# Expert layer: the last layer norm moved beside the eighth expert's products, its rows patched by gather and scatter

## The chip, the cores and the metric

The kernel runs on one core of a Trainium2 chip. The metric is the device time of one execution in microseconds (us). Engines: PE is TensorE (its weight load is PEld), DVE is VectorE, ACT is ScalarE, POOL is GpSimd; SP issues DMAs, and POOL issues the indirect ones (gathers and scatters by a list of row numbers).

## The reference

```
x = x + cross_attention(layernorm(x), ctx)          # 4 x 1024 tokens of 256
hidden = layernorm(x)
# mixture of experts on hidden, 8 experts, each token goes to its best two
scores = softmax(hidden @ wg); gates, idx = top_k(scores, 2); gates /= sum(gates)
pos = place of the token in its expert's list (1280 places an expert)
h = silu(disp @ fc1_w.T + fc1_b)                    # 256 -> 1024
y = h @ fc2_w + fc2_b                               # 1024 -> 256
res = hidden + sum over the two experts of gate * y[pos]
x = x + (res - mean(res)) * rsqrt(var(res) + 1e-5) * ln_gamma + ln_beta
```

All data are 32-bit floats; the 4096 tokens are 32 tiles of 128 rows.

## The kernel before, in words

**Stages.** Attention fills most of the first 290 us and leaves `X` (residual rows, in SBUF, 32 tiles) and two copies in DRAM of the normalised rows: `xn_rows`, from which experts gather, and `sum_rows`, onto which their results are added. Routing then makes `slot_ids`: for each slot the row numbers to gather and to scatter (empty places scatter to rows beyond the 4096th).

**Expert stage.** Each of 8 experts has `SPE` = 5 slots of 256 places, so there are `NST` = 40 slots, numbered 0 to 39; slots 35 to 39 are the eighth expert's. `expert_steps` runs a step c = 0 to 42 on PE, ACT and DVE, each engine taking its own list in order. In step c PE transposes the gathered rows of slot c+1, makes the first product of slot c (`fc1`), and then the second product of slot c-1 (`fc2`, two halves of 128 rows, each into its own bank, `YB` and `YB`+1). A half may only begin when DVE has read the bank of the slot before (`y_made`). ACT makes `xT_hi` (`rows_hi`), silu (`hraw`), and multiplies the results of slot c-2 by their gates (`scale_results`, `y_scaled`). DVE adds the bias to the results of slot c-2 (line 1687), makes `xT_lo` of slot c+1 (line 1669), splits `hraw` into `h_hi` (line 1699) and `h_lo` (line 1701), and splits weights of the next expert. A product is three matmuls (`mm3`, lines 897 to 899) of such high and low parts. Slots that lie wholly or by half beyond the expert's tokens skip their products (line 1235 stands in).

**POOL** runs its own loop: in turn `st` it gathers the rows of slot `st`+4 (line 599, two indirect DMAs), scatters slot `st`-2 with addition onto `sum_rows` (line 611, two) and, up to `st` = 31, adds `beta_sb` to a tile of `X`. SP loads the next expert's weights (`w1raw`, `w2raw`).

**Last stage.** When all scatters have landed, SP loads `sum_rows` into `res` in nine DMAs and layer norm runs over 8 groups of 4 tiles (`QT`, `NQ`): ACT makes the statistics of the first two tiles, DVE those of the last two (lines 1725, 1729); POOL raises the variance to the power -0.5 (line 658); DVE (lines 1735, 1741) or ACT (line 887), POOL (gamma, line 663) and DVE (line 1747) scale the rows and add `X`; SP stores `z` to `out`.

Of the kernel before, what the change touches and what calls it, by code (L numbers as in the profile page):

```python
# [5 lines left out]
def xattn_moe_kernel(nc, x, ctxT, wqT, bq, wkT, bk, wvT, bv, woT, wo, bo, boT, wg, w1T, b1T, w2, b2, gamma, beta, out):  # L6
# [50 lines left out]
    sum_rows = nc.dram_tensor("sum_rows", [N + 4 * P, D], f32, kind="Internal").ap()  # L57
    x_t = x.rearrange("(t p) d -> p t d", p=P)
# [24 lines left out]
    with root:  # L83
        def sb(name, shape, dt=f32, where=root):
# [20 lines left out]
        my_row = sb("my_row", [P, 1])  # L105

# [85 lines left out]
        w1_hi, w1_lo = sb("w1_hi", [P, 2, DC, HID], f32r, M), sb("w1_lo", [P, 2, DC, HID], f32r, M)  # L192
        w2_hi, w2_lo = sb("w2_hi", [P, 2, HJ, D], f32r, M), sb("w2_lo", [P, 2, HJ, D], f32r, M)
# [12 lines left out]
        res = sb("res", [P, NT, D], f32, C)  # L206
        z = sb("z", [P, NT, D], f32, C)
        unused, squares = sb("unused", [P, 2, D], f32, C), sb("squares", [P, 2, D], f32, C)
        st_d, mv_d = sb("st_d", [P, NT, 6], f32, C), sb("mv_d", [P, NT, 2], f32, C)
        m16_d, nmu_d, var_d, vare_d, rstd_d, nmr_d = (sb(n, [P, NT], f32, C)  # L210
                                                      for n in ("m16_d", "nmu_d", "var_d", "vare_d", "rstd_d", "nmr_d"))
        eps_d, zero_d = sb("eps_d", [P, QT], f32, C), sb("zero_d", [P, QT], f32, C)
        C.close()

        def halves_in_order():

            for k in range(1, NQ + 2):
                if k <= NQ:
                    yield QT * (k - 1) + 2
                if k >= 2:  # L220
                    yield QT * (k - 2)
# [9 lines left out]
        for name in (  # L231
# [7 lines left out]
            "xT_hi_made h_made y_scaled w_hi_made z_made mean16_made act_stats_made "  # L239
# [7 lines left out]
            "h_hi_made h_lo_made y_made st3_made mv3_made var3_made nmr_made z_scaled_dve out_made"  # L247
# [19 lines left out]
        stored = dma_sem("stored")  # L267

# [110 lines left out]
        def _(sp):  # L379
# [46 lines left out]
            sp.wait_ge(scattered[0], 32 * (NST // 2))  # L426
            sp.wait_ge(scattered[1], 32 * (NST // 2))
# [4 lines left out]
            for g, a in enumerate(halves_in_order()):  # L432
                sp.wait_ge(sem("out_made"), g + 1)
                sp.dma_start(out_t[:, a:a + 2, :], z[:, a:a + 2, :]).then_inc(stored, 16)
            sp.wait_ge(stored, 16 * (NT // 2))


        @block.gpsimd
        def _(pool):
# [27 lines left out]
            g.memset(ones_f[:], 1.0).then_inc(sem("zero_made"), 1)  # L467
            pool.wait_ge(sem("masks_made"), 3)
# [134 lines left out]
            def scatter(st):  # L603

                if within(st, NST):
# [3 lines left out]
                    for q in range(2):  # L609
# [3 lines left out]
                                             compute_op=ALU.add).then_inc(scattered[u], 16)  # L613

# [39 lines left out]
            for k in range(NQ + 1):  # L654
                if k < NQ:
                    quad = slice(QT * k, QT * (k + 1))
                    pool.wait_ge(sem("var3_made"), k + 1)
                    g.tensor_tensor(rstd_d[:, quad], vare_d[:, quad], minus_half[:, 0:QT], ALU.pow)\
                        .then_inc(sem("rstd3_made"), 1)
                if k >= 1:  # L660
                    for t in (QT * (k - 1), QT * (k - 1) + 1):
                        pool.wait_ge(sem("z_made"), 2 * (k - 1) + t % QT + 1)
                        g.tensor_tensor(z[:, t, :], z[:, t, :], gamma_sb[:], ALU.mult).then_inc(sem("z_scaled"), 1)
# [3 lines left out]
        def _(act):  # L667
# [166 lines left out]
            def scale_results(gq, c):  # L834
                if within_st(gq, c):
                    e = 2 * gq + c // SPE
                    for q in range(2):
                        act.wait_ge(sem("y_made"), 2 * (10 * gq + c) + q + 1)
                        y = y_sb[:, c % 2, q, :]
                        a.activation(y, y, ACT.Copy, scale=xg[:, c % XR, q, ds(D + e, 1)]).then_inc(sem("y_scaled"), 1)  # L840

            def expert_step(gq, c):
                rows_hi(gq, c + 1)
                if within_st(gq, c):
                    st = 10 * gq + c
# [7 lines left out]
                scale_results(gq, c - 2)  # L853
                e, s = 2 * gq + c // SPE + 1, c % SPE
# [6 lines left out]
            def first_two(k):  # L861

                if k < NQ:
                    a0 = QT * k
                    for t in (a0, a0 + 1):
                        res_loaded(act, t)
                        a.activation(unused[:, t % 2, :], res[:, t, :], ACT.Copy, scale=1.0 / (16 * D),
                                     accum_out=m16_d[:, t:t + 1]).then_inc(sem("mean16_made"), 1)
                    act.wait_ge(sem("mean16_made"), 2 * (k + 1))
                    a.activation(nmu_d[:, a0:a0 + 2], m16_d[:, a0:a0 + 2], ACT.Copy, scale=-16.0)\  # L870
                        .then_inc(sem("act_stats_made"), 1)
                    for t in (a0, a0 + 1):
# [4 lines left out]
            first_two(0)
            first_two(1)
            for k in range(NQ):
                first_two(k + 2)  # L880
                act.wait_ge(sem("rstd3_made"), k + 1)
                for t in (QT * k, QT * k + 1):
                    a.activation(nmr_d[:, t:t + 1], nmu_d[:, t:t + 1], ACT.Copy, scale=rstd_d[:, t:t + 1])\
                        .then_inc(sem("nmr_made"), 1)
                act.wait_ge(sem("nmr_made"), 2 * (k + 1))
# [912 lines left out]
```

## Time and profile before

| what | value |
|---|---|
| median of 3 runs | 766.76 us (766.38 to 767.35) |
| span of the profiled execution | 769.2 us (no other time is listed for it) |
| PE busy | 680.1 us, 88% of the span |
| DVE busy | 564.4 us, 73% |
| ACT busy | 406.3 us, 53% |
| POOL busy | 430.1 us, 56% |
| DMA | 64.10 MB, mean 83 GB/s |

The busy time of an engine says how much work it has over the whole span; which of them sets the end differs by stage and is read from the chain of waits and from windows of the span. Times of rows are counted from the start of the span.

### The profile page before, as it was taken

The page shows a single profiled execution, that of the slowest core. Times are in us where ns is not written, and L with a number is a line of the kernel's source. Part 1 is how long each engine was busy: PE and PEld are TensorE (multiplying, and loading weights), DVE is VectorE, ACT ScalarE, POOL GpSimd, SP SyncE. Part 2 cuts the span into 40 slices and gives each one's busy share as a digit, 9 for nine tenths or more (in the row PEclk, how much of TensorE's full clock was granted, in tenths as well). Part 3 has the DMA queues.
Part 4 walks back from the last instruction along what each step waited for, and adds up shares of the span by engine and source line. Part 5 has one row for each costly group of instructions (what it writes and reads, how often), then busy time and mean ns, then how long its engine had stood idle before and what let it go on. Part 6 is the DMA issues. An engine that isn't in the chain of part 4 may idle for free.

```text
span 769.2 us, 15696 instructions
## 1 busy us (share of the span) xinstructions
PE 680.1 (88%) x5592; PEld 649.1 (84%) x5592; DVE 564.4 (73%) x1198; ACT 406.3 (53%) x955; POOL 430.1 (56%) x547
## 2 busy tenths in 40 slices
PE   5999999999999834999999999999999999999500
PEld 4789999998988723999999999999999999999500
DVE  5589898988888797665565679777696666854187
ACT  3356555555555594454454467455464454643185
POOL 6744665565564334436445558766576554632456
PEclk9699999999999955999999999999999999999855
DMA  9501101011010122434344446544455343322484
GB/s 295 176 15 43 42 28 43 30 41 43 29 43 29 42 85 65 149 84 94 51 107 69 81 106 123 125 96 73 98 123 114 46 101 52 58 29 28 64 266 150
DMA packets 55764, 64.10 MB, mean 83 GB/s; under 512 B 9472, under 2 KB 50944, under 8 KB 55552
## 3 DMA queue, kind: packets, MB, share of 16 engines
q0 software_dynamic: 15360, 21.31, 17.1%
q1 hardware_dynamic: 39616, 41.64, 16.6%
q8 instruction: 55, 0.90, 0.5%
q14 instruction: 29, 0.24, 0.1%
q10 hardware_dynamic: 704, 0.01, 0.0%
HBM read 39.22 MB, written 23.72 MB: 82 GB/s over the span
## 4 chain that ended last, share of the span: by engine, by line
PE 81%; DVE 11%; issue 3%; DMA 2%; ACT 1%; POOL 1%; POOLq 0%; SPq 0%; DVEq 0%; ACTq 0%
PE banks L897 18%; PE banks L899 18%; PE banks L898 18%; PE banks L1039 8%; PE banks L1025 5%; PE banks L1013 5%; PE banks L1171 2%; PE banks L1075 1%; PE banks L920 1%; DVE oh_lo L1485 1%; PE banks L942 1%; DVE oh_id L1481 1%; DVE z L1741 1%; DMA res<-sum_rows 1%; DVE z L1735 1%
## 5 line engine op out<-in xcount | busy, mean ns | idle before, releaser
L611 POOL DMA_INDIRECT sum_rows<-y_sb,slot_ids x80 | 131.4, 1643 | 162.1 <-ACT y_sb L840 145.4
L850 ACT ACTIVATE hraw<-banks,b_now 128x256 f32<-128x256 f32 x320 | 132.2, 477 | 90.3 <-PE banks L899 80.5
L897 PE MATMUL banks<-xT_hi,w_hi 128*128 128x256 f32 x560 | 161.6, 289 | 1.7 <-ACT xT_hi L822 1.7
L899 PE MATMUL banks<-xT_hi,w_lo 128*128 128x256 f32 x560 | 158.5, 283 | 0.0
L898 PE MATMUL banks<-xT_lo,w_hi 128*128 128x256 f32 x560 | 158.4, 283 | 0.0
L897 PE MATMUL banks<-w_hi,h_hi 128*128 128x256 f32 x528 | 148.8, 282 | 1.3 <-issue 1.3
L898 PE MATMUL banks<-w_lo,h_hi 128*128 128x256 f32 x528 | 148.6, 281 | 0.0
L899 PE MATMUL banks<-w_hi,h_lo 128*128 128x256 f32 x528 | 148.5, 281 | 0.0
L1701 DVE TENSOR_TENSOR h_lo<-hraw,h_hi 128x512 fp32r<-128x512 f32 x160 | 114.6, 716 | 5.5
L1699 DVE CAST h_hi<-hraw 128x512 fp32r<-128x512 f32 x160 | 77.5, 485 | 45.8 <-ACT hraw L850 44.6
L897 PEld LDWEIGHTS banks<-xT_hi,w_hi 128*128 128x128 f32 x560 | 106.3, 190 | 2.2 <-issue 2.1
L599 POOL DMA_INDIRECT xg<-xn_rows,slot_ids x80 | 89.8, 1122 | 30.3 <-issue 29.4
L898 PEld LDWEIGHTS banks<-xT_lo,w_hi 128*128 128x128 f32 x560 | 106.4, 190 | 0.2 <-issue 0.2
L899 PEld LDWEIGHTS banks<-xT_hi,w_lo 128*128 128x128 f32 x560 | 106.2, 190 | 0.0
L897 PEld LDWEIGHTS banks<-w_hi,h_hi 128*128 128x128 f32 x528 | 99.4, 188 | 1.8 <-issue 1.8
L899 PEld LDWEIGHTS banks<-w_hi,h_lo 128*128 128x128 f32 x528 | 99.4, 188 | 0.0
L898 PEld LDWEIGHTS banks<-w_lo,h_hi 128*128 128x128 f32 x528 | 99.4, 188 | 0.0
L738 ACT ACTIVATE probsT<-banks 124x384 f32<-124x384 f32 (+1 forms) x128 | 55.8, 436 | 70.9 <-PE banks L1025 70.8
L822 ACT ACTIVATE xT_hi<-banks 128x512 fp32r<-128x512 f32 x40 | 24.1, 602 | 114.2 <-PE banks L1171 106.3
L1039 PE MATMUL banks<-VB,probsT 124*128 124x51 f32 (+2 forms) x640 | 82.7, 268 | 0.0
L1039 PEld LDWEIGHTS banks<-VB,probsT 124*128 124x128 f32 x640 | 81.4, 192 | 0.0
L574 POOL TENSOR_TENSOR rstd<-var,minus_half 128x1 f32<-128x1 f32 x32 | 17.6, 550 | 96.3 <-DVE var L1580 96.3
(216 smaller groups left out, 1442.7 us busy)
## 6 DMA issues: line engine op xcount, KB each, us to landing
w1raw<-in_w1T SPq DMA_DIRECT2D x8, 1024.0 KB
w2raw<-in_w SPq DMA_DIRECT2D x8, 1024.0 KB
xn_rows<-xn SPq DMA_DIRECT2D x32, 128.0 KB, 1.8
sum_rows<-xn SPq DMA_DIRECT2D x32, 128.0 KB, 1.8
out<-z SPq DMA_DIRECT2D x16, 256.0 KB, 2.2
res<-sum_rows SPq DMA_DIRECT2D x7, 512.0 KB, 8.5
X<-in_x SPq DMA_DIRECT2D x2, 1280.0 KB, 12.1
xg<-xn_rows,slot_ids POOLq DMA_INDIRECT x80
```

Of the source, the lines that this page charges most:

```text
L599: g.indirect_dma_start(xg[:, st % XR, q, :], None, xn_rows, bass.IndirectOffsetOnAxis(ap=slot_ids[:, st, 0, q:q + 1], axis=0), bounds_chec ...
L611: g.indirect_dma_start(sum_rows, bass.IndirectOffsetOnAxis(ap=slot_ids[:, st, 1, q:q + 1], axis=0), y_sb[:, u, q, :], None, bounds_check=N ...
L738: a.activation(probsT[:, j0:j0 + w, :].rearrange("r j q -> r (j q)"), banks[0:JW, PT, 0:w * P], ACT.Copy).then_inc(sem("pT_made"), 1)
L850: a.activation(hraw[:, j // 2, j % 2, :], banks[:, j // 2, (j % 2) * 256:(j % 2 + 1) * 256], ACT.Silu, bias=b1_now[:, (c // SPE) % 2, j:j ...
L897: t_.matmul(o, a_hi, b_hi, start=first, stop=False)
L898: t_.matmul(o, a_hi, b_lo, start=False, stop=False)
L899: return t_.matmul(o, a_lo, b_hi, start=False, stop=last)
L1013: m = t_.matmul(banks[:, 2 * f + h, 0:KC], qq[rows, f, qs], kk[rows, ds((2 * b + f) * KH + h * KC, KC)], start=(n == 0), stop=(n == 2))
L1025: m = t_.transpose(banks[0:JW, PT, (j - j0) * P:(j - j0 + 1) * P], probs[:, 1 - u, f * KH + j * JS:f * KH + j * JS + JW], ident[:])
L1039: m = t_.matmul(banks[:, PV, f * VW + a_:f * VW + a_ + n_], probsT[:, NJ * f + j, :], VB[:, ds(((2 * b + f) * NJ + j) * VW + a_, n_)], sta ...
L1699: v.tensor_copy(hi, raw).then_inc(sem("h_hi_made"), 1)
L1701: v.tensor_tensor(lo, raw, hi.bitcast(f32), ALU.subtract).then_inc(sem("h_lo_made"), 1)
```

## The change

The last stage is taken apart. (1) The rows of the seven first experts' sums (`sum_rows` after slot 34) are loaded and normalised in the steps c = 36 to 40 of the eighth expert (`FIRST_SLOT` = 36): `wave_step(k)` on DVE, two groups of four tiles a step, `first_normalised` on ACT, `deviations` and `first_scaled` on POOL, and all rows are stored to `out`. (2) The eighth expert's results are not scattered. For its 10 half slots POOL gathers the sums of those rows (`gather_sums`) and the rows of `X` with beta (`gather_rest`, from `rest_rows`, a new copy in DRAM that SP writes during the expert stage); DVE adds gate times result to the gathered sums (`patch_sum`), normalises them after its last step (`patch_begun`, `patch_done`), and POOL scatters them over their rows of `out` (`scatter_patch`) after all the other stores. (3) Besides: for slots 35 to 39 ACT makes `h_hi` instead of DVE, and the bias `b2` enters as a matmul with a row of ones; the statistics of two tiles come from one instruction over 512 interleaved elements, for all tiles on DVE; the buffers for this lie where weights lay.

```diff
@@ sync
+                sp.wait_ge(sem("beta_added"), QT * e)
+                sp.dma_start(rest_t[:, ds(QT * (e - 1), QT), :], X[:, ds(QT * (e - 1), QT), 0:D]).then_inc(rests_stored, 16)
...
+            for u in range(2):
+                sp.wait_ge(scattered[u], 32 * ((SL + 1 - u) // 2))
...
             for n, (a, b) in enumerate(RES_LOADS):
-                sp.dma_start(res[:, a:b, :], sum_t[:, a:b, :]).then_inc(load_res[n], 16)
+                sp.dma_start(wave(a, b), sum_t[:, a:b, :]).then_inc(load_res[n], 16)
...
+            for n, a in enumerate(pairs_in_order()):
+                store_pair(n, a)
             sp.wait_ge(stored, 16 * (NT // 2))
+            sp.wait_ge(patched, 16 * 2 * SPE)
@@ gpsimd
-                if within(st, NST):
+                if within(st, SL):
...
+                if 0 <= st - SL + 2 < SPE:
+                    gather_rest(st - SL + 2)
...
+            for u in range(2):
+                pool.wait_ge(scattered[u], 32 * ((SL + 1 - u) // 2))
+            for m in range(SPE):
+                gather_sums(m)
+            deviations(0)
+            deviations(1)
+            for k in range(NQ):
+                deviations(k + 2)
+                first_scaled(k)
+            patch_deviations(0)
+            patch_deviations(1)
+            pool.wait_ge(stored, 16 * (NT // 2))
+            for m in range(SPE):
+                scatter_patch(m)
+                patch_deviations(m + 2)
@@ scalar
+                if c == SL + 1:
+                    scale_results(c - 2)
...
+                        if st >= SL and j % 2 and j > 1:
+                            activation_hi(st, j // 2 - 1)
...
+                k = 2 * (c - FIRST_SLOT - 1)
+                if 0 <= k < NQ:
+                    first_normalised(k)
+                    first_normalised(k + 1)
@@ tensor
+                        if e == LAST:
+                            pe.wait_ge(load_b2, 16)
+                            pe.wait_ge(sem("zero_made"), 3)
+                            t_.matmul(o, ones_row[:], b2_sb[0:1, e, :], start=True, stop=False)
@@ vector
+            def quad_begun(k):
+                a = QT * k
+                for n in (2 * k + 1, 2 * k):
+                    pair_stats(n)
+                dve.wait_ge(sem("st3_made"), 2 * k + 2)
+                v.tensor_scalar(var_d[:, a:a + QT].rearrange("p (a b) -> p a b", b=2), st_d[:, 2 * k:2 * k + 2, :, 2],
+                                1.0 / D, EPS_LN, ALU.mult, ALU.add).then_inc(sem("var3_made"), 1)
+                for t in (a + 2, a + 3):
+                    z = row_of(wave(t, t + 1))
+                    v.scalar_tensor_tensor(z, z, st_d[:, t // 2, t % 2, 1:2], gamma_sb[:], ALU.subtract, ALU.mult)\
+                        .then_inc(sem("z_scaled_dve"), 1)
...
+            def wave_step(k):
+                if k < NQ:
+                    quad_begun(k)
+                    quad_begun(k + 1)
+                    first_bias(k)
+                    last_done(k)
+                if k >= 2:
+                    first_done(k - 2)
+                    first_done(k - 1)
+                if k < NQ:
+                    first_bias(k + 1)
+                    last_done(k + 1)
...
+            def patch_sum(c):
+                if c == SL:
+                    dve.wait_ge(sums_gathered, 16 * 2 * SPE)
+                for q in range(2):
+                    dve.wait_ge(sem("fc2_done" if q else "fc2_half_done"), c + 1)
+                    r = row_of(patch(2 * (c - SL) + q, 2 * (c - SL) + q + 1))
+                    v.scalar_tensor_tensor(r, banks[:, YB + q, 0:D], xg[:, c % XR, q, D + LAST:D + LAST + 1], r,
+                                           ALU.mult, ALU.add).then_inc(sem("y_made"), 1)
...
             def expert_step(gq, c):
...
+                elif within_st(gq, c - 2):
+                    patch_sum(c - 2)
                 rows_lo(gq, c + 1)
...
+                if c == FIRST_SLOT:
+                    dve.wait_ge(sem("beta_added"), NT)
+                k = 2 * (c - FIRST_SLOT)
+                if 0 <= k < NQ + 2:
+                    wave_step(k)
...
+            patch_begun(0)
+            for m in range(SPE):
+                if m + 1 < SPE:
+                    patch_begun(m + 1)
+                patch_done(m)
```

`first_bias` is one small DVE instruction that waits for `deviations` of its group, `last_done` two of 128x256 behind it, `first_done` one of 128x512 that waits for `first_scaled`. `patch_begun` is a statistics instruction over 128x512, a small one, and two of 128x256; `patch_done` two of 128x256 that wait for `patch_deviations`.

## Rows read from the trace of the kernel before

**Rows 1.** Busy time of each engine (and its instructions), clock and DMA in two stretches
```profile
710.00:722.50 12.50, 12.47 (x106) 12.26 (x104) 3.88 (x8) 3.76 (x9) 7.25 (x5) 1.00 0.38 43
722.50:769.20 46.70, 0.00 (x0) 0.00 (x0) 31.60 (x89) 28.52 (x105) 24.87 (x26) 0.52 0.59 186
```
**Rows 2.** The chain that ended last, from the last product: start, us, what
```profile
722.51 0.43 DVE y_sb L1687
...
724.23 3.79 DMA sum_rows<-y_sb,slot_ids
...
729.02 5.52 DMA res<-sum_rows
...
764.95 0.69 DVE z L1747
```
**Rows 3.** Timeline of DVE in slots 34 to 36: start, us, instruction, idle before
```profile
671.58 0.75 DVE L1687 TENSOR_TENSOR y_sb<-banks,b_sb 128x256 f32<-128x256 f32 x2
...
677.47 0.69 DVE L1701 TENSOR_TENSOR h_lo<-hraw,h_hi 128x512 fp32r<-128x512 f32 x1
678.99 0.42 DVE L1687 TENSOR_TENSOR y_sb<-banks,b_sb 128x256 f32<-128x256 f32 x1 [0.83 <-PE banks L899]
...
690.80 0.42 DVE L1687 TENSOR_TENSOR y_sb<-banks,b_sb 128x256 f32<-128x256 f32 x1 [0.82 <-PE banks L899]
693.59 0.42 DVE L1687 TENSOR_TENSOR y_sb<-banks,b_sb 128x256 f32<-128x256 f32 x1 [2.36 <-PE banks L899]
```
**Rows 4.** Timeline of POOL, turns 33 to 36 of its loop
```profile
657.33 1.57 POOL L611 DMA_INDIRECT sum_rows<-y_sb,slot_ids  x1 [0.30 <-issue]
659.20 1.08 POOL L599 DMA_INDIRECT xg<-xn_rows,slot_ids  x1 [0.30 <-issue]
...
663.88 1.84 POOL L611 DMA_INDIRECT sum_rows<-y_sb,slot_ids  x1 [2.02 <-ACT y_sb L840]
...
671.62 1.72 POOL L611 DMA_INDIRECT sum_rows<-y_sb,slot_ids  x1 [0.91 <-ACT y_sb L840]
673.65 1.79 POOL L611 DMA_INDIRECT sum_rows<-y_sb,slot_ids  x1 [0.31 <-issue]
678.13 1.56 POOL L611 DMA_INDIRECT sum_rows<-y_sb,slot_ids  x1 [2.69 <-ACT y_sb L840]
680.00 1.55 POOL L611 DMA_INDIRECT sum_rows<-y_sb,slot_ids  x1 [0.30 <-issue]
```
**Rows 5.** Instructions of the last stage by line and form: count, busy us, mean ns
```profile
L663 POOL TENSOR_TENSOR z<-z,gamma_sb 128x256 f32<-128x256 f32 x16 | 13.4, 860 | 5.7 <-ACT z L887 5.7
L658 POOL TENSOR_TENSOR rstd_d<-vare_d,minus_half 128x4 f32<-128x4 f32 x8 | 9.5, 1183 | 10.7 <-DVE vare_d L1733 10.7
L1741 DVE SCALAR_TENSOR_TENSOR z<-z,rstd_d,X 128x256 f32<-128x256 f32 x16 | 8.8, 591 | 0.0
...
L1735 DVE SCALAR_TENSOR_TENSOR z<-res,mv_d,gamma_sb 128x256 f32<-128x256 f32 x16 | 7.4, 505 | 0.0
...
L1747 DVE TENSOR_TENSOR z<-z,X 128x512 f32<-128x512 f32 x8 | 6.0, 746 | 0.6 <-POOL z L663 0.6
L1725 DVE BATCH_NORM_STATS2 st_d<-res 128x6 f32<-128x256 f32 x16 | 6.0, 412 | 9.3 <-DMA res<-sum_rows 9.3
...
L1733 DVE TENSOR_SCALAR vare_d<-var_d 128x2 f32<-128x2 f32 x8 | 1.3, 160 | 1.1 <-ACT squares L873 0.9
```
**Rows 6.** Timeline of POOL, one of the first gathers of the expert stage
```profile
298.85 1.01 POOL L599 DMA_INDIRECT xg<-xn_rows,slot_ids  x1 [0.31 <-issue]
```
**Rows 7.** Timeline of PE, start of the expert stage
```profile
304.81 0.55 PE L897 MATMUL banks<-xT_hi,w_hi 128*128 128x256 f32 x1 [1.72 <-ACT xT_hi L822]
```
**Rows 8.** Windows there, columns as in rows 1 (the last but two is the clock)
```profile
307.00:308.00 1.00, 1.00 (x7) 1.00 (x6) 0.00 (x0) 0.00 (x0) 0.91 (x1) 0.50 0.92 352
309.00:310.00 1.00, 1.00 (x11) 1.00 (x11) 0.00 (x0) 0.00 (x0) 0.70 (x2) 1.00 1.00 387
```
**Rows 9.** The chain in the attention stage: three plain 32-bit matmuls of up to 51 columns
```profile
149.95 0.32 PE banks L1039 x3
```

More of the change, by code:

```diff
@@ L205, in xattn_moe_kernel, with flat, wave, row_of @@
         RES_LOADS = [(0, 2), (2, 4)] + [(QT * k, QT * (k + 1)) for k in range(1, NQ)]
[L206 to L221, printed above, removed]
+        LAST = NE - 1
+        SL = LAST * SPE
+        FREE = 1 - LAST % 2
+        FIRST_SLOT = SL + 1
+        assert NT == 32 and HJ == 8 and LAST * SPE >= NT and XR == 2 * SPE and FREE == 0
+        def flat(ap):
+            return ap.rearrange("p c h -> p (c h)").rearrange("p (t d) -> p t d", d=D)
+        spare = [flat(w1raw[:]), w2raw[:]] + [late_rows[:, 8 * n:8 * n + 8, :] for n in range(4)]
+        def wave(a, b):
+            return spare[a // 8][:, a % 8:a % 8 + b - a, :]
+        def row_of(tiles):
+            return tiles.rearrange("p t d -> p (t d)")
+        def patch(a, b):
+            return spare[4 + a // 8][:, a % 8:a % 8 + b - a, :]
+        def rest(n):
+            return xg[:, n // 2, n % 2, 0:D]
         banks = root.enter_context(nc.psum_tensor("banks", [P, 8, 512], f32))
@@ L651, in _, with deviations @@
                     g.tensor_tensor(X[:, st, 0:D], X[:, st, 0:D], beta_sb[:], ALU.add).then_inc(sem("beta_added"), 1)
-            for k in range(NQ + 1):
+                if 0 <= st - SL + 2 < SPE:
+                    gather_rest(st - SL + 2)
+            def deviations(k):
                 if k < NQ:
@@ L877, in _ @@
[L877 to L885, printed above, removed]
-                for t in (QT * k, QT * k + 1):
-                    a.activation(z[:, t, :], res[:, t, :], ACT.Identity, scale=rstd_d[:, t:t + 1],
-                                 bias=nmr_d[:, t:t + 1]).then_inc(sem("z_made"), 1)
@@ new lines, in first_bias, with last_done @@
+            def first_bias(k):
+                a = QT * k
+                dve.wait_ge(sem("rstd3_made"), k + 1)
+                v.scalar_tensor_tensor(nmr_d[:, a:a + 2], st_d[:, 2 * k, :, 1], -1.0, rstd_d[:, a:a + 2],
+                                       ALU.mult, ALU.mult).then_inc(sem("nmr_made"), 1)
+            def last_done(k):
+                dve.wait_ge(sem("rstd3_made"), k + 1)
+                dve.wait_ge(sem("z_scaled_dve"), 2 * k + 2)
+                for t in (QT * k + 2, QT * k + 3):
+                    z = row_of(wave(t, t + 1))
+                    m = v.scalar_tensor_tensor(z, z, rstd_d[:, t:t + 1], X[:, t, 0:D], ALU.mult, ALU.add)
+                m.then_inc(sem("out_made"), 1)
@@ new lines, in patch_begun @@
+            def patch_begun(m):
+                two = slice(2 * m, 2 * m + 2)
+                dve.wait_ge(sem("y_made"), 2 * (SL + m + 1))
+                v.bn_stats(st_p[:, m].rearrange("p a b -> p (a b)"), patch(2 * m, 2 * m + 2).rearrange("p t d -> p d t"))\
+                    .then_inc(sem("st3_made"), 1)
+                dve.wait_ge(sem("st3_made"), NT // 2 + m + 1)
+                v.tensor_scalar(var_p[:, two], st_p[:, m, :, 2], 1.0 / D, EPS_LN, ALU.mult, ALU.add)\
+                    .then_inc(sem("var3_made"), 1)
+                for q in range(2):
+                    r = row_of(patch(2 * m + q, 2 * m + q + 1))
+                    v.scalar_tensor_tensor(r, r, st_p[:, m, q, 1:2], gamma_sb[:], ALU.subtract, ALU.mult)\
+                        .then_inc(sem("z_scaled_dve"), 1)
@@ new lines, in patch_done @@
+            def patch_done(m):
+                if m == 0:
+                    dve.wait_ge(rests_gathered, 16 * 2 * SPE)
+                dve.wait_ge(sem("rstd3_made"), NQ + m + 1)
+                for q in range(2):
+                    n = 2 * m + q
+                    dve.wait_ge(sem("z_scaled_dve"), NT // 2 + n + 1)
+                    r = row_of(patch(n, n + 1))
+                    v.scalar_tensor_tensor(r, r, rstd_p[:, n:n + 1], rest(n), ALU.mult, ALU.add)\
+                        .then_inc(sem("out_made"), 1)
```

204 lines of the change are left out of this document (119 added, 85 removed).

## The prediction

> **What bounds the kernel now.** I read the busy time by windows first, then the chain of waits at the end, then the timelines of DVE and POOL in the last expert. Up to 722.5 us PE is busy all the time at the full granted clock, and DVE, ACT and POOL are each busy for less than 60% [rows 1]: the expert stage goes at PE's pace. From 722.5 to 769.2, 46.7 us, PE does nothing [rows 1]. The chain there is the last result (722.5), its scatter (landed 3.8 us after its start), the load of the sums (5.5), and then the layer norm on DVE to 765.6 [rows 2]. The change can win at most a part of these 46.7 us, and what it moves ahead of 722.5 costs nothing only as long as PE isn't held. So two questions decide: how long is the new tail, and how long does PE wait in slots 35 to 39?
>
> On DVE's timeline the results of slot 34 come at 671.6, those of 35 from 679.0, of 36 from 690.8 [rows 3]. A slot takes 11.8 us, a half of `fc2` 2.8 us (690.80 to 693.59); `fc2` of slot 36 starts at about 688.0 [rows 3].
>
> **The change part by part. (1) POOL's queue up to the sums.** `gather_rest` adds two gathers to each of turns 33 to 37, six of them ahead of slot 34's scatter. The work of turns 34 and 35 runs from 659.2 to 675.4 with waits of 2.02 and 0.91 us ahead of two scatters [rows 4]; of these, 0.30 each is the usual gap, the other 2.3 us fill up. Six gathers at 1.08 + 0.30 are 8.3 us. So 675.4 - 2.3 + 8.3 = 681.4. Slot 34's results are ready by then (671.58 and 0.75 on DVE, then ACT's scaling, which the change moves ahead of its silu), so its second scatter starts at 681.4 + 0.3 + 1.56 + 0.3 = 683.6 instead of 680.0 [rows 4], and lands 3.8 us later [rows 2], at 687.4. `gather_rest` of the last two turns (4 x 1.38) holds POOL until about 690.9, and only then come the ten `gather_sums`. Their price: 1.31 with DVE idle [rows 6] to 1.38 beside a busy DVE [rows 4]; DVE is idle here (below), so 13.1 us, to 704.0. Behind them in POOL's order stand `deviations(0)` and `deviations(1)`, 1.18 each [rows 5] and about 0.1 to start: 705.3 and 706.6.
>
> **(2) The first wave holds DVE, and DVE holds PE.** DVE finishes the split of slot 36 at about 678.2 [rows 3] and enters `wave_step(0)`. There it waits for the first loads, which cannot land before 687.4 + 6.5 (the first two issues and the 5.5 us of the load on the chain [rows 2]), about 694, and then for POOL's `deviations`: `first_bias(1)` at 706.7, 0.16 and two of 0.5 behind it [rows 5], done at 708.0. Behind it on DVE stands `patch_sum` of slot 35, which frees the bank that `fc2` of slot 36 needs: 708.0 + 0.42 [rows 3] = 708.4 against 688.0 before. PE stands for 20.4 us. The gathered sums (last start 702.7, 3.8 us by the scatter's landing) are there in time, 706.5.
>
> **(3) Waves 2, 4 and 6.** One wave is two groups. DVE's part by row means [rows 5]: four statistics instructions over 512 elements, which before doesn't show: 0.75 (line 1747, the same elements) to 0.82 (twice line 1725), I take 0.75, so 3.0; small ones 4 x 0.16; four of line 1735 and four of line 1741, 2.0 and 2.4; two of line 1747, 1.5. In all 9.5 us, less the overlap of neighbours (two instructions of 0.42 take 0.75, 0.09 apiece [rows 3]), about 8.3. POOL's part, in its order power, two by gamma, power, two by gamma, is 2 x (1.18 + 2 x 0.86) = 5.8 [rows 5]; it starts when the first group's variance is there (some 1.7 into the wave), ends at 7.5, and `first_done` and `last_done` of the second group come behind it on DVE, 1.9: 9.4 us. I take 9.4. The bounds are 7.9 (all of DVE's 31.6 us of the old stage over eight groups [rows 1]) and 9.4 plus what POOL and DVE do to each other (below). Between the waves DVE does `patch_sum` (0.75), `xT_lo` and four `h_lo` at 0.6 net of overlap [rows 3]: 3.8 us, in step 39 without `xT_lo` 3.2. That is 13.2 us a step against PE's 11.8 and 1.0 of bias: DVE sets the pace. `patch_sum` of slot 38 frees its bank at 708.0 + 2 x 13.2 + 3.2 + 9.4 + 0.4 = 747.4.
>
> **(4) The last product.** Two halves of 2.8, and two bias matmuls. Those are plain 32-bit: 51 columns take 0.107 [rows 9], 256 scaled 0.54; the lower bound is the pace of `fc2`, 2.8 / 24 = 0.12; I take 0.5, together 1.0. PE has stood for about 6 us before it (its `fc2` of slot 38 starts at about 735 and takes 6.6). After the last product of before the granted clock falls to 1.2 GHz (mean 0.52 of 2.4 over the 46.7 us, so at most 2 us of them full [rows 1]). At the start of the expert stage PE restarts at 304.8 [rows 7], and the clock is still 0.50 in the window at 307 and 1.00 at 309 [rows 8]: about 3 us at half pace, 1.5 lost. So 747.4 + 5.6 + 1.0 + 1.5 = 755.5. After the 20 us stand the same 1.5 is lost, but DVE is then the slower one.
>
> **(5) The new tail.** `patch_sum` 0.42; `patch_begun` twice, each 0.75, 0.26 and two of 0.4 net: 3.6; half of `patch_done` 0.5: the first patched half is ready at 760.0. Then POOL: ten scatters and three powers among them. A scatter without addition isn't in the trace: the gather 1.38, the adding scatter 1.56 + 0.30 [rows 4]; I take 1.38, as the addition is what falls away. The power of 128x2 is priced as that of 128x4, 1.18. The last scatter starts at 760.0 + 9 x 1.38 + 3.5 = 775.9, lands 3.8 later, and the end is about 1 us behind (765.64 to 769.2 held a store's issue, landing and the end [rows 1, 2]): 780.7. The tail is 25 us instead of 46.7; 33 us of waits (20.4, and the steps 37 to 39 at DVE's pace with slot 39's end) pay for it.
>
> **Costed at nothing.** The stores to `rest_rows` (4 MB more) run beside products in stretches where the DMA engines are about 0.4 busy [rows 1]; SP's weight loads stand behind them, but POOL's four beta turns an expert run ahead of the five slots, and a load is used most of an expert (5 x 11.8 us) after its issue; if that cover were gone, each expert would wait for a store, some microseconds. `h_hi` on ACT in the last expert: ACT is busy for 3.8 of 12.5 us [rows 1]; four casts a slot at about 0.7 fit. ACT's statistics and POOL's share of the old stage fall away with the tail.
>
> **Sum.** 780.7 against the span of 769.2: 11.5 us more. The profiled execution was 2.4 us longer than the median 766.76; carried to it: **778 us**. Its own bounds: waves at 7.9, bias 0.12 and no clock loss give 7 us less, 771; scatters at 1.86 and statistics at 0.82 give 5 more, to which waits on POOL may add 2: 785.
>
> **A rule beside a row.** Line 1741 takes 591 ns where line 1735, of the same shape and with the same number of tensor inputs, takes 505 [rows 5]: 0.09 us more when POOL multiplies. The Trainium skill (SBUF — State Buffer, "Who interferes with whom") says that a DVE instruction with two SBUF inputs and a GpSimd instruction that reads SBUF exclude each other for the whole instruction. By the row the price is in the means already; by the rule it could be far larger, and that is the second rival.
>
> **The rivals.** *Faster: indirect DMAs cost POOL less when they come in a row.* Ten gathers of rests, ten of sums and ten scatters stand on the path. At 0.7 each, POOL would be through by 694 and the first wave would end with the loads, about 698, 10 us sooner; the scatters give 6 more: 764.5 of span, 762 us. It decides from about 0.95 each. Against: ten in a row in the expert stage's start cost 1.01 + 0.30, no less [rows 6]. *About the same: the rests cost no time on the path*, because POOL's waits in earlier turns take them up; slot 34 lands at 681, the gathers start then: 10 us less, 768. Against: in turns 34 and 35 POOL waits for only 2.3 us that could be filled [rows 4]. *Slower still: POOL and DVE exclude each other in the waves.* If none of POOL's four multiplications a wave overlaps with DVE, 4 x 0.86 [rows 5] a wave: 10.3 us more in three waves, 788. For it: the 591 against 505; against it: the mean moved by 0.09 only.
>
> **How the numbers follow.** My sum (771 to 785) 0.56; exclusion or dearer scatters beyond it 0.23; rests at no cost 0.10 (0.07 of it within 0.2%, the rest on either side); cheap indirect DMAs or what else ends faster 0.11. About 0.2% (1.5 us) is what a measurement can tell from no change. Faster 0.12, within it 0.07, slower 0.81. The range that holds 8 in 10 reaches from 767 to 790: about 0.14 lies below and 0.06 above.
>
> **What would show it.** Right: the load of the sums starts about 687; ten gathers in a row on POOL to about 704; PE idle from 688 to 708; steps of about 13 us on DVE; PE's last product ends near 755; a tail of 25 us in which POOL scatters. Wrong: `fc2` of slot 36 before 700; waves under 8 us, so that PE has no second gap; or gathers below 1 us.

## The result, and the profile after

| kernel | median | lowest to highest | ratio to before (95% interval) |
|---|---|---|---|
| before (4 runs) | 766.78 us | 766.38 to 767.35 | |
| after (4 runs) | 786.69 us | 784.6 to 789.23 | 1.0253 (1.0236 to 1.0271) |

The change makes the kernel 19.9 us, 2.5%, slower. The forecast was 778 (767 to 790): right in direction, for the reason that it gave, and short by 8.7 us.

First, which clock the rows are on. The profiled execution of after took 785.83 us and its span is 784.1, so the time is the span and 1.7 us. Three later runs of before show the same (768.3 with a span of 766.6, 766.61 with 764.9, 767.93 with 766.2). By that, the profiled execution of before, with its span of 769.2, took about 770.9 us, some 4 more than the median; the prediction took it to be 2.4. In after, slot 31's scatter starts at 654.11 and not at 657.33 [rows 4], so to set the forecast beside the rows of after, 3.2 us are taken off each of its times.

POOL's timeline of after (start, us, engine, line, instruction, idle before), from slot 34's second scatter to the first wave:

```profile
681.06 1.57 POOL L658 DMA_INDIRECT sum_rows<-y_sb,slot_ids  x1 [0.30 <-issue]
682.94 1.08 POOL L668 DMA_INDIRECT xg<-rest_rows,slot_ids  x1 [0.30 <-issue]
...
688.25 1.00 POOL L674 DMA_INDIRECT late_rows<-sum_rows,slot_ids  x1 [0.30 <-issue]
...
699.98 1.00 POOL L674 DMA_INDIRECT late_rows<-sum_rows,slot_ids  x1 [0.30 <-issue]
701.00 2.04 POOL L724 TENSOR_TENSOR rstd_d<-var_d,minus_half 128x4 f32<-128x4 f32 x2
```

The scatter that stood at 680.00 in before [rows 4] has six gathers of rests ahead of it, four more behind it (to 687.95), and then the ten gathers of sums. Only at 701 does POOL reach the two powers for which the first wave waits. DVE's timeline of after shows the waits that follow:

```profile
689.60 1.30 DVE L1780 BATCH_NORM_STATS2 st_d<-w1raw 128x6 f32<-128x512 f32 x2 [12.47 <-DMA w1raw<-sum_rows]
...
702.10 0.16 DVE L1799 SCALAR_TENSOR_TENSOR nmr_d<-st_d,rstd_d 128x2 f32<-128x2 f32 x1 [7.64 <-POOL rstd_d L724]
...
705.17 0.88 DVE L1836 SCALAR_TENSOR_TENSOR late_rows<-banks,xg,late_rows 128x256 f32<-128x256 f32 x2 [1.13 <-DMA late_rows<-sum_rows,slot_ids]
...
716.71 0.69 DVE L1813 TENSOR_TENSOR w1raw<-w1raw,X 128x512 f32<-128x512 f32 x1 [1.32 <-POOL w1raw L731]
...
718.18 0.87 DVE L1836 SCALAR_TENSOR_TENSOR late_rows<-banks,xg,late_rows 128x256 f32<-128x256 f32 x2
718.97 0.68 DVE L1767 TENSOR_TENSOR xT_lo<-banks,xT_hi 128x512 fp32r<-128x512 f32 x1
720.75 0.69 DVE L1888 TENSOR_TENSOR h_lo<-hraw,h_hi 128x512 fp32r<-128x512 f32 x1 [1.10 <-ACT h_hi L945]
722.17 0.69 DVE L1888 TENSOR_TENSOR h_lo<-hraw,h_hi 128x512 fp32r<-128x512 f32 x1 [0.73 <-ACT h_hi L945]
723.60 1.29 DVE L1888 TENSOR_TENSOR h_lo<-hraw,h_hi 128x512 fp32r<-128x512 f32 x2 [0.73 <-ACT h_hi L945]
...
734.04 0.87 DVE L1836 SCALAR_TENSOR_TENSOR late_rows<-banks,xg,late_rows 128x256 f32<-128x256 f32 x2
...
748.08 0.86 DVE L1836 SCALAR_TENSOR_TENSOR late_rows<-banks,xg,late_rows 128x256 f32<-128x256 f32 x2
...
758.06 0.48 DVE L1836 SCALAR_TENSOR_TENSOR late_rows<-banks,xg,late_rows 128x256 f32<-128x256 f32 x1 [3.17 <-PE banks L993]
```

Line 1836 is `patch_sum`, which frees the bank for PE: 705.17, 718.18, 734.04 and 748.08, then the last half at 758.06. What PE does meanwhile, from its timeline:

```profile
705.87 1.19 PE L1326 MATMUL banks<-b_sb,ones_row 1*128 1x256 f32 x2 [19.58 <-issue]
```

and from the windows (busy time and instructions of PE, PEld, DVE, ACT, POOL; then the granted clock, the DMA share and GB/s):

```profile
706.00:708.00 2.00, 2.00 (x6) 1.35 (x7) 2.00 (x5) 0.00 (x0) 0.00 (x0) 0.50 0.00 1
710.00:712.00 2.00, 2.00 (x11) 2.00 (x11) 1.97 (x6) 0.00 (x0) 1.45 (x2) 0.50 0.00 0
712.00:714.00 2.00, 2.00 (x14) 1.53 (x13) 1.97 (x6) 0.00 (x0) 1.89 (x3) 1.00 0.00 0
...
750.00:752.00 2.00, 2.00 (x10) 2.00 (x11) 0.64 (x2) 0.00 (x0) 0.00 (x0) 0.50 0.51 175
```

PE stands for 19.58 us, then works for 6.1 us at a clock of 0.50 (1.2 GHz), and does so again for some 4 us after a second gap, 742.46 to 748.76. The prediction had read 3 us from the start of the expert stage [rows 7, 8]. The end of POOL's timeline of after, and SP's waits there:

```profile
763.03 1.07 POOL L744 DMA_INDIRECT out<-late_rows,slot_ids  x1 [1.14 <-DVE late_rows L1860]
764.40 0.99 POOL L744 DMA_INDIRECT out<-late_rows,slot_ids  x1 [0.30 <-issue]
...
777.28 0.97 POOL L744 DMA_INDIRECT out<-late_rows,slot_ids  x1 [0.30 <-issue]
```

```profile
SPq L85 <- PEq L85: 4.1, 1, 4.1
```

The old tail of 46.7 us [rows 1] has become one of 26.0 (758.06 to 784.1), as forecast; the 20.7 us won are paid nearly twice over ahead of it: the last product ends 38.8 us later than before's (758.06 against 722.5, with 3.2 taken off). By steps, the forecast (3.2 us taken off) beside after:

| step | forecast | after | off by, in this step |
|---|---|---|---|
| slot 34's second scatter starts | 680.4 | 681.06 | +0.7 |
| ten gathers of sums end | 700.8 | 700.98 | -0.5 |
| first wave ends | 704.8 | 704.04 | -0.9 |
| `patch_sum` of 35 starts | 704.8 | 705.17 | +1.1 |
| of 36 | 718.0 | 718.18 | -0.2 |
| of 37 | 731.2 | 734.04 | +2.7 |
| of 38 | 743.8 | 748.08 | +1.4 |
| last product ends | 752.3 | 758.06 | +1.5 |
| end of the span | 777.5 | 784.1 | +0.8 |

That is 6.6 us. The median of after is 0.9 above its profiled run, and 3.2 off and 1.7 on instead of 2.4 off are another 0.9: with the rounding, the 8.7.

### The profile page after: what moved, and what is told of

Same layout as the page of the kernel before. It is cut to its first block, busy times and chain, and to the rows that moved or that the text cites. A ratio compares the mean times of both kernels' runs of the same rounds, so it can differ in the third digit from the quotient of the medians.

```text
span 784.1 us, 15739 instructions
## 1 busy us (share of the span) xinstructions
PE 690.3 (88%) x5612; PEld 654.5 (83%) x5612; DVE 567.3 (72%) x1192; ACT 391.9 (50%) x877; POOL 445.4 (57%) x573
## 4 chain that ended last, share of the span: by engine, by line
PE 81%; DVE 8%; issue 6%; POOL 2%; ACT 1%; DMA 0%; POOLq 0%; DVEq 0%; ACTq 0%
PE banks L991 19%; PE banks L993 18%; PE banks L992 18%; PE banks L1133 8%; PE banks L1119 5%; PE banks L1107 4%; PE banks L1265 2%; PE banks L1169 1%; PE banks L1014 1%; PE banks L1326 1%; DVE oh_lo L1583 1%; DVE oh_id L1579 1%; PE banks L1036 1%; POOL out L744 1%; DVE h_lo L1888 1%
## 5 line engine op out<-in xcount | busy, mean ns | idle before, releaser
L658 POOL DMA_INDIRECT sum_rows<-y_sb,slot_ids x70 | 113.5, 1621 | 133.4 <-ACT y_sb L938 117.5
L991 PE MATMUL banks<-w_hi,h_hi 128*128 128x256 f32 x528 | 151.9, 288 | 1.5 <-issue 1.3
L992 PE MATMUL banks<-w_lo,h_hi 128*128 128x256 f32 x528 | 150.3, 285 | 0.0
L993 PE MATMUL banks<-w_hi,h_lo 128*128 128x256 f32 x528 | 150.1, 284 | 0.0
L1888 DVE TENSOR_TENSOR h_lo<-hraw,h_hi 128x512 fp32r<-128x512 f32 x160 | 112.1, 705 | 13.2 <-ACT h_hi L945 8.4
L991 PEld LDWEIGHTS banks<-w_hi,h_hi 128*128 128x128 f32 x528 | 101.2, 192 | 6.2 <-issue 5.9
L646 POOL DMA_INDIRECT xg<-xn_rows,slot_ids x80 | 87.1, 1088 | 30.5 <-issue 19.4
L992 PEld LDWEIGHTS banks<-w_lo,h_hi 128*128 128x128 f32 x528 | 101.3, 192 | 0.0
L993 PEld LDWEIGHTS banks<-w_hi,h_lo 128*128 128x128 f32 x528 | 101.1, 192 | 0.0
L1884 DVE CAST h_hi<-hraw 128x512 fp32r<-128x512 f32 x140 | 70.9, 506 | 38.4 <-ACT hraw L965 37.9
```

Source lines behind the costliest of these rows:

```text
L646: g.indirect_dma_start(xg[:, st % XR, q, :], None, xn_rows, bass.IndirectOffsetOnAxis(ap=slot_ids[:, st, 0, q:q + 1], axis=0), bounds_chec ...
L658: g.indirect_dma_start(sum_rows, bass.IndirectOffsetOnAxis(ap=slot_ids[:, st, 1, q:q + 1], axis=0), y_sb[:, u, q, :], None, bounds_check=N ...
L991: t_.matmul(o, a_hi, b_hi, start=first, stop=False)
L992: t_.matmul(o, a_hi, b_lo, start=False, stop=False)
L993: return t_.matmul(o, a_lo, b_hi, start=False, stop=last)
L1884: v.tensor_copy(hi, raw).then_inc(sem("h_hi_made"), 1)
```

## The experiments

All ten are edits of the changed kernel, each measured beside the kernel before. "Gain" is the difference of its ratio to 1.0253, times 766.8 us.

**e1: the gathers of rests behind the waves.** POOL's queue up to the first wave is ten instructions shorter; nothing else changes.

```diff
-                if 0 <= st - SL + 2 < SPE:
-                    gather_rest(st - SL + 2)
...
                 first_scaled(k)
+                for m in {1: (0, 1), 3: (2, 3), 5: (4,)}.get(k, ()):
+                    gather_rest(m)
```

> All ten gathers of rests move on POOL from the turns around slot 34's scatter to behind the second, fourth and sixth gamma multiplication, where POOL waits anyway. Theory (POOL's queue up to the tenth sum gather and its powers sets the end of the first wave): slot 34's second scatter starts about 6 us sooner, the first sum gather about 10 us sooner, PE's long gap shrinks from 19.6 to about 10 us and the time falls by 9 to 10 us, to 777. Rival (the waves hold PE at DVE's pace whatever the start, so the PE gap only moves to later steps): less than 4 us.

Measured: 777.19 us, 1.0143 (1.0103 to 1.0182), a gain of 8.4 us. The ten gathers of sums start at 680.99, the first wave is through and `patch_sum` of slot 35 runs at 698.71, and PE's gap is 12.03 us instead of 19.58: 7.5 us of the gain are there. POOL's queue sets the first wave; the rests were not free.

**e2 and e3: only slot 35's gathers ahead of the first wave**, each slot with a semaphore of its own; e3 is e1 and e2 together.

```diff
-            for m in range(SPE):
-                gather_sums(m)
+            gather_sums(0)
             deviations(0)
             deviations(1)
+            for m in range(1, SPE):
+                gather_sums(m)
```

> Only the two sum gathers of slot 35 stand ahead of the first two powers on POOL, the other eight behind them, and each patched sum waits for its own two gathers. Theory: the first wave ends about 8 us sooner and PE's long gap is about 11 us; the eight gathers then delay the powers of the second wave, so the time falls by 5 to 8 us, to 779 to 782. Rival (the loads of the sums, not POOL, hold the first wave): under 2 us.

> Both of these. Theory: the first wave ends about 14 us sooner, limited then by the loads; PE's long gap is 4 to 6 us; 770 to 774. Rival (DVE's pace): not below 778.

Measured: e2 783.81 us, 1.0221 (1.0186 to 1.0256), a gain of 2.5, less than the 5 to 8 expected and not clear of noise, as its interval reaches the 1.0253 of after; e3 775.11 us, 1.0117 (1.0085 to 1.0149), a gain of 10.4, just short of the 770 to 774 us expected. The gap of PE shrinks to 10.25 us in e2 and 5.25 in e3, but the gathers that were put off now stand between POOL's work of the next wave. DVE's timeline of e2, the first row of line 1800 behind slot 35's `patch_sum`:

```profile
709.98 0.70 DVE L1800 SCALAR_TENSOR_TENSOR nmr_d<-st_d,rstd_d 128x2 f32<-128x2 f32 x1 [4.18 <-POOL rstd_d L724]
```

In these two orders POOL is the late engine in the second wave as well: moving a transfer behind the first moves the wait.

**e4: the waves a step later as well** (`FIRST_SLOT = SL + 2`), so that slot 35's `patch_sum` has no wave ahead of it.

> Both, and the waves start one step later (step 37), when the loads have landed, so that DVE never waits for a load ahead of work that PE needs. Theory: PE has no gap over 3 us, its last product ends some 3 to 6 us later than before's, the last wave and the patches follow it: 756 to 763, faster than both kernels. Rival (DVE's pace of 13 us a step holds PE): 770 or more.

Measured: 774.05 us, 1.0104 (1.0074 to 1.0133), a gain of 11.4. My theory fell. PE's gap is down to 2.16 us, 17.4 us less than in after, but the time falls by only 11.4: 6 us are lost again, and DVE's timeline of e4 shows where.

```profile
686.99 0.88 DVE L1836 SCALAR_TENSOR_TENSOR late_rows<-banks,xg,late_rows 128x256 f32<-128x256 f32 x2 [11.72 <-DMA late_rows<-sum_rows,slot_ids]
701.03 0.88 DVE L1836 SCALAR_TENSOR_TENSOR late_rows<-banks,xg,late_rows 128x256 f32<-128x256 f32 x2 [4.01 <-DMA late_rows<-sum_rows,slot_ids]
```

DVE stands for 11.72 us for slot 35's gathers and does no wave meanwhile, and waits again for the late ones. Four steps with a wave each, 11.5 to 14.0 us long, still have to follow, and the same tail behind them. With PE's gap closed, DVE's own list sets the end.

**e5: PE kept busy in its two gaps** by 150 and 45 products into a bank that nothing reads; what is computed stays as it is. This prices the clock alone.

```diff
+                        for _ in range({SL + 1: 150, SL + 4: 45}.get(st, 0)):
+                            t_.matmul(banks[:, 7, 0:256], w1_hi[w][:, 0, 0:P], w1_lo[w][:, 0, 0:256], start=True, stop=True)
                         wait(pe, sem("y_made"), 2 * st - 1)
```

> The changed kernel, with 150 matmuls into an unused bank at the start of PE's 19.6 us gap and 45 at the start of its 6.3 us gap, so that PE is busy at full clock when its wait ends; nothing else moves. Theory (the half clock behind the gaps is on the path: it makes the first product of slot 38 late for DVE's split, and slows the last product): the step from slot 36's patched sum to slot 37's shrinks from 15.9 to about 13.2 us, the last product from 9.5 to about 7, and the time falls by 4 to 5 us, to 782. Rival (DVE sets the pace in steps 37 and 38 whatever PE's clock, as predicted): only the last product's 2 us, 785.

Measured: 781.87 us, 1.0181 (1.0163 to 1.0198), a gain of 5.5 us with the same gathers and waves. One window of e5, where after had a clock of 0.50:

```profile
706.00:708.00 2.00, 2.00 (x15) 1.53 (x14) 2.00 (x5) 0.00 (x0) 0.00 (x0) 1.00 0.28 96
```

It is 1.00. DVE's timeline of e5 in the step that was too long:

```profile
719.00 0.87 DVE L1838 SCALAR_TENSOR_TENSOR late_rows<-banks,xg,late_rows 128x256 f32<-128x256 f32 x2
...
720.38 2.49 DVE L1890 TENSOR_TENSOR h_lo<-hraw,h_hi 128x512 fp32r<-128x512 f32 x4
...
732.04 0.87 DVE L1838 SCALAR_TENSOR_TENSOR late_rows<-banks,xg,late_rows 128x256 f32<-128x256 f32 x2
```

The four `h_lo` follow each other without a wait. `patch_sum` starts at 705.98, 719.00, 732.04 and 746.12 and the last half at 754.09: steps of 13.0, 13.0 and 14.1 us and 8.0 for the last product, where after has 13.0, 15.9, 14.0 and 10.0. So the first stretch at half clock cost 2.8 us and the second 2.0, and none of it was hidden by DVE.

**e6: the order that e4 showed.** Later waves, all sums gathered first, the powers behind them, eight rests in the stretch in which POOL waits for the waves, the last two behind group 1.

```diff
-        FREE = 1 - LAST % 2
-        FIRST_SLOT = SL + 1
+        FREE = 1 - LAST % 2
+        FIRST_SLOT = SL + 2
...
             deviations(1)
+            for m in range(SPE - 1):
+                gather_rest(m)
             for k in range(NQ):
...
                 first_scaled(k)
+                if k == 1:
+                    gather_rest(SPE - 1)
```

> As the run with waves one step later, but POOL gathers all sums first, then the first two powers, then eight gathers of rests where it waited for the second wave, the last two behind the second wave. Theory (in that run DVE stood 4 us for a gather that POOL issued late, and POOL's six late gathers of rests held the last waves): the second patched sum comes at about 697 instead of 701, the last wave ends near 735 instead of 744: 760 to 765. Rival (with DVE's own work as the limit, the waves take 9 us each whatever POOL does): 770 or more.

Measured: 771.55 us, 1.005 (1.0033 to 1.0066), a gain of 15.6; the rival held by its number. PE's gap is 3.17 us and eight of POOL's rests lie where POOL would wait. What is left shows on DVE's timeline of e6:

```profile
690.25 0.88 DVE L1837 SCALAR_TENSOR_TENSOR late_rows<-banks,xg,late_rows 128x256 f32<-128x256 f32 x2 [12.71 <-DMA late_rows<-sum_rows,slot_ids]
...
700.18 0.48 DVE L1837 SCALAR_TENSOR_TENSOR late_rows<-banks,xg,late_rows 128x256 f32<-128x256 f32 x1
...
705.73 0.69 DVE L1889 TENSOR_TENSOR h_lo<-hraw,h_hi 128x512 fp32r<-128x512 f32 x1 [2.97 <-ACT h_hi L947]
...
719.09 0.87 DVE L1837 SCALAR_TENSOR_TENSOR late_rows<-banks,xg,late_rows 128x256 f32<-128x256 f32 x2
732.07 0.87 DVE L1837 SCALAR_TENSOR_TENSOR late_rows<-banks,xg,late_rows 128x256 f32<-128x256 f32 x2
743.13 0.86 DVE L1837 SCALAR_TENSOR_TENSOR late_rows<-banks,xg,late_rows 128x256 f32<-128x256 f32 x2
```

It stands for 12.71 us until slot 35's sums are there, though they were issued at 681.43: the nine loads of `sum_rows` (4 MB) have the DMA engines at the same time. The steps from there are 9.9, 18.9, 13.0 and 11.1 us. In the one of 18.9 DVE waits 4.4 us (2.97, 0.73 and 0.73) for `h_hi` of slot 38, as in after, and PE, back from its gap at 690.94, works at a clock of 0.50 to 696.8. So not only DVE's own work is left.

**e7: the last addition of a wave put behind its other work**, so that DVE doesn't stand 1.3 us for POOL.

```diff
                     first_done(k - 2)
-                    first_done(k - 1)
                 if k < NQ:
...
                     last_done(k + 1)
+                if k >= 2:
+                    first_done(k - 1)
```

> The same, and in each wave the addition that waits for POOL's second gamma multiplication comes last on DVE, behind the second group's own rows, with the stores in that order. Theory (1.3 us of wait a wave are POOL's): three waves 1.3 us shorter, 3 to 4 us less than without it, 757 to 762. Rival (POOL is the limit of a wave): no difference.

Measured: 771.46 us, 1.0044 (1.0028 to 1.006); against e6 nothing, as the rival had it. The wait of DVE falls from 1.33 to 0.64 us, but POOL's two multiplications beside it grow, and so does the small `first_bias` of DVE. POOL's timeline of e7, the two pairs of one wave, and DVE's in the second:

```profile
712.53 1.43 POOL L730 TENSOR_TENSOR w1raw<-w1raw,gamma_sb 128x256 f32<-128x256 f32 x2
...
715.23 3.03 POOL L730 TENSOR_TENSOR w1raw<-w1raw,gamma_sb 128x256 f32<-128x256 f32 x2
```

```profile
716.16 0.70 DVE L1802 SCALAR_TENSOR_TENSOR nmr_d<-st_d,rstd_d 128x2 f32<-128x2 f32 x1
716.79 0.87 DVE L1810 SCALAR_TENSOR_TENSOR w2raw<-w2raw,rstd_d,X 128x256 f32<-128x256 f32 x2
```

Beside a statistics instruction of DVE, with one input, a pair takes 1.43 us (1.41 in after); beside instructions with two SBUF inputs 2.31 in after and 3.03 here. DVE's pairs of 128x256 take 0.87 or 0.88 there, but the 128x2 instruction takes 0.70 us and not its 0.15: of the 0.69 us of wait that the order saves, 0.55 come back in it.

**e8 and e9: e6 with the first loads spread and PE kept warm.** In e8 the loads of `sum_rows` from the fourth on wait until slot 35's sums have landed, and 12 products into the unused bank stand ahead of slot 36's `fc2`; e9 has 26 of these products and no pacing. What is computed stays as it is.

```diff
             for n, (a, b) in enumerate(RES_LOADS):
+                if n == 3:
+                    sp.wait_ge(sums_gathered[0], 32)
```

> As the run with the gathers in POOL's idle window; besides, SP issues the loads of the sums from the fourth on only when slot 35's two gathers have landed, and PE runs 12 matmuls into an unused bank ahead of the wait of slot 36's second product. Theory (the gathers took 7 us to land beside the loads, and the half clock behind the 3 us gap made slot 38's split late by 4 us): the first patched sum comes 3 us sooner, DVE's waits for slot 38's split fall from 4.4 to under 1 us, the time falls by 5 to 7 us to 764 to 767, about before's. Rival (POOL's work in the waves sets the end): under 2 us.

> As that, with 26 such matmuls and no pacing of the loads. Theory: the clock alone is worth 3 to 4 us, 768. Rival: under 1 us.

Measured: e8 767.7 us, 0.9999 (0.9985 to 1.0012), a gain of 19.5 in all and 3.9 over e6, where 5 to 7 were expected; e9 769.86 us, 1.0024 (1.001 to 1.0038), 2.0 over e6, where 3 to 4 were expected. In e8 slot 35's `patch_sum` runs at 687.17 instead of 690.25, 6.4 us behind the issue of its first gather (680.79) instead of 8.8: 2.4 of the gain. The rest lies in the steps from there to slot 39's `patch_sum`, 51.5 us instead of 52.9; in e9 they take 50.8. The clock stays at 1.00 in both, yet DVE still waits 3.1 and 2.8 us for slot 38's `h_hi`, and not under 1: the half clock was only a part of those 4.4 us. With both edits the whole loss is undone, and the kernel is level with the one before. What the 12 products of e8 give beside the pacing no run separates.

**e10: e8 with the first half of three patches moved into the steps.**

```diff
+                if c == SL + 3:
+                    patch_begun(0)
...
                     first_done(k - 2)
+                    if 4 <= k < NQ:
+                        patch_begun(k // 2 - 1)
                     first_done(k - 1)
```

> Edit: as the paced and warmed version (767.7 us, 0.9999 of the kernel before), and besides the statistics and the first scaling of the patches of slots 35, 36 and 37 are moved from behind the last expert step to places in the steps in which VectorE waits (slot 35's after the lower halves of slot 38's rows, those of 36 and 37 in the waves ahead of their last addition), their powers on POOL behind the waves' multiplications. The computation is that of the changed kernel. Theory: what stands behind the last matrix product is then only the last two patches' statistics, so the tail of about 25.6 us shrinks by 4 to 5 us, and the time is 762 to 764 us, faster than the kernel before by 0.5 per cent. Rival: VectorE's 1.3 us for each moved patch lengthen the waves by as much as the tail loses, or the tail is set by POOL's ten scatters and their wait for the stores, not by VectorE's patches: within 1 us of 767.7.

Measured: 767.1 us, 1.0003 (0.999 to 1.0017): the rival held, by both of its ways. From slot 35's `patch_sum` to slot 39's it is 53.1 us (686.22 to 739.34) and in e8 51.5 (687.17 to 738.68): 1.6 of the moved work came back. Behind it, POOL's timeline of e10 shows the limit:

```profile
744.58 1.07 POOL L744 DMA_INDIRECT out<-late_rows,slot_ids  x1 [4.58 <-DVE late_rows L1867]
...
758.10 0.97 POOL L744 DMA_INDIRECT out<-late_rows,slot_ids  x1 [0.30 <-issue]
```

The wait of 4.58 is put down to line 1867, but the first half of its work is done by 741.8; by the code the first scatter also waits for the last store, which follows line 1819 at 741.4. From `patch_sum` of slot 39 to the first scatter it is 5.2 us (7.1 in e8), from there to the last scatter 13.5 (14.2), and from the last scatter's start to the end 6.8 in both. The ten scatters must follow the last store, and they are 14 to 15 us of POOL in either version. No version here beats the kernel before.

## Why the prediction was right, and where its sizes were off

**The place and the mechanism held.** POOL's queue, lengthened by ten gathers of rests, sets the first wave; DVE stands in the wave and `patch_sum` behind it holds the bank; PE stands 19.58 us against 20.4 forecast; the tail is 26.0 against 25.2. e1 shortened POOL's queue, the first link, and gained 8.4 us. What DVE takes for a wave, 9.2 us (708.96 to 718.18) against 9.4, and the first step at DVE's pace, 13.0 against 13.2, are as forecast too. So is the sign, for the reason given: 20.7 us won at the end, 38.8 lost ahead of it.

**The step that failed: "After the 20 us stand the same 1.5 is lost, but DVE is then the slower one."** Both halves were wrong. PE works at half clock for 6.1 us, not 3, which makes slot 36's `fc2` 3 us later; and DVE is not the slower one, since its next work behind the wave is `h_lo` of slot 38, which comes out of PE's products through ACT: three waits of 1.10, 0.73 and 0.73 in the step that ends at 734.04, 2.6 of the 2.7 us that it is over. In e5 these waits are gone, and the step is 13.0. The forecast had DVE's list and PE's list as rivals for the pace of a step; in one step they stand behind each other.

The 3 us were read from PE's restart at 304.81 [rows 7]. PE's timeline of before shows that this was not its first work behind the gap there:

```profile
301.97 1.12 PE L1171 MATMUL banks<-ident,xg 128*128 128x128 f32 x4 [6.95 <-DMA xg<-xn_rows,slot_ids]
```

From 301.97 to the rise of the clock at 308.0 it is 6.0 us, with a wait of 1.7 in it, as long as in after.

**Sizes.** *The last product* was put at 8.1 us with 1.5 for the clock; it took 9.5 from the freeing of its banks, some 4 us of it at half clock, and e5 gives 2.0 back. *The last wave* took 10.2 us (737.83 to 748.08), 1.0 over the others (its cause is below, with the rivals); ahead of it 0.5 went to a wait for `h_hi` on ACT, so that edit was not quite free. *The gathers of sums* were put at the scatter's 3.8 us to landing; beside the loads they took 5.2 to 6.6 (median 6.0), and DVE waited 1.13 for them. *The end* was put at about 1 us behind the last landing; after has a wait of 4.1 there, between the queues of SP and PE, before 1.1 in the same view (`SPq L83 <- PEq L83`). The other way: a gather in a row on POOL takes 1.00 + 0.30 with DVE idle, not 1.01 + 0.30, and a scatter without addition 0.97 to 1.24 (1.05 in the mean) + 0.30, near the 1.38 taken, and 2.4 to landing, less than 3.8; two statistics of 128x512 take 1.31, as 0.66 and not 0.75 each; and a power of 128x2 takes 0.74 to 0.86, not 1.18.

**Bias matmul.** Two take 0.66 to 0.69 us at full clock and 1.19 at half; the bounds were 0.12 and 0.54 for one, 0.5 was taken: 0.34.

**The rivals.** *Cheap indirect DMAs* fell: none was under 0.97 + 0.30, against the 0.95 from which it decides. *Rests at no cost* fell with e1 in this order of POOL's work, while e6 shows another order in which they delay little. *Exclusion of POOL and DVE* is there, on both engines. In after a pair of POOL's multiplications takes 2.31 us beside DVE's instructions with two SBUF inputs and 1.42 beside its statistics, and DVE waits 1.32 us a wave for it: 3.9 in three waves, inside the 9.4 forecast for each. DVE's own instructions grow as well: line 1789, 128x4, takes 0.62 to 0.64 beside a multiplication and 0.17 without, and a pair of 128x256 that else takes 0.87 takes 1.94 in e8 (708.86). In the last wave, where four multiplications stand on POOL in a row, DVE's timeline of after has

```profile
745.57 1.20 DVE L1813 TENSOR_TENSOR late_rows<-late_rows,X 128x512 f32<-128x512 f32 x1 [1.29 <-POOL late_rows L731]
746.69 0.68 DVE L1799 SCALAR_TENSOR_TENSOR nmr_d<-st_d,rstd_d 128x2 f32<-128x2 f32 x1
```

against 0.69 and 0.15 in the waves ahead, which is the 1.0 us over. In e1, where two gathers stand between those multiplications, the same two take 0.69 and 0.15 and the last wave 9.2. The prediction held "the mean moved by 0.09 only" against this rival, but a mean hides it. Line 1741 of before, with its shortest, median and longest in ns:

```profile
L1741 DVE SCALAR_TENSOR_TENSOR z<-z,rstd_d,X x16: 472/473/946, 737.6 to 762.3; 128x256 f32<-128x256 f32 x16
```

Most take 473 and some twice that; a mean of 591 is that of twelve and four. The rival's 788 lies nearer to the result than 778 does, but by luck: the waves take 9.2, 9.2 and 10.2 us where 9.4 was summed, so at most 0.8 of the missing 8.7 us is its own, and 3.3 are the clock's by e5 (2.8, and 2.0 where 1.5 was taken). The Trainium skill (SBUF — State Buffer, "Who interferes with whom") has just this line: a DVE instruction with two SBUF inputs contends with a GpSimd instruction that reads SBUF, and one with at most one input, outside the modes that use both ports, doesn't. The trace agrees for POOL's pairs, 2.31 and 3.03 against 1.42; line 1789 has one SBUF input and is held even so, and no run here shows which mode it runs in.

**The clock.** That PE comes back at 1.2 GHz after a gap is in rows of both kernels; that it was on the path is shown by e5. A short gap does it too: in e4 PE stands for 2.16 us, and the windows behind it read

```profile
689.00:690.00 1.00, 1.00 (x7) 1.00 (x6) 1.00 (x3) 0.00 (x0) 0.00 (x0) 0.50 1.10 347
...
692.00:693.00 1.00, 1.00 (x9) 0.87 (x8) 0.96 (x5) 0.00 (x0) 0.62 (x1) 1.00 0.85 277
```

0.50 from 688 on and 1.00 again at 692. So e4 and e6, which close most of PE's gap, still pay for the clock behind it; e9, with the clock at 1.00 throughout, gains 2.0 us over e6.

## What to carry to other kernels

Work taken from an idle tail must be laid on the engine that issues it in the order in which others wait for it: here ten small transfers, each 1.3 us of POOL, moved the time by 8 us by their place in the queue alone. When a gap opens on TensorE, price the clock behind it as well, and look for what the next engine in line takes from TensorE's late products before calling it hidden. Read the shortest and the longest of a row and not its mean, before a rival is dropped. And before a tail is overlapped, count what must still come last: the ten scatters behind the last store and what stands round them left 26 of 47 us. In e8 the tail is 18.6 us shorter than in before (28.1 against 46.7), and the last result comes 18.5 us later, counted from slot 31's second scatter: that is why it only drew level.

## What was not expected of the hardware

- How long TensorE works at 0.50 of its clock behind a gap does not follow the length of the gap: 6.1 us after 19.6 (705.9 to 712.0 in after), 4.1 after 6.3 (748.8 to 752.9), 3.7 after 2.16 (e4), 5.9 after 3.17 (e6). In e7, after 3.13 us, it came back at 1.00 (691.98) and fell to 0.50 only from 693.4 to 696.8, while it was busy. Why these differ no run here tells.
- DVE and POOL hold each other up in the layer norm: 473 ns become 946 on an instruction of DVE in the kernel before, and 1.42 us become 2.31 and 3.03 on a pair of POOL's multiplications.
- Gathers issued beside 4 MB of loads landed after 6.0 us (median), scatters without addition at the end after 2.4.
- The last wait of SP for PE's queue is 4.1 us in after and in all ten edits of it, and 1.1 in the kernel before: 3.0 us of the changed kernel's tail that no order of its work touched. No run here tells why; it stays open.
